# The last expert layer of a four-layer model: twelve token tiles sorted by expert, and router products over repeated columns

## The reference

```python
h = h + _L0_ffn_ref(_layernorm(h), ...)     # 8 experts, the best 2 for each token
h = h + _L2_ffn_ref(_layernorm(h), ...)     # 8 experts, weights of the best 2
h = h + _L3_attn_ref(_layernorm(h), ...)
h = h + _L3_ffn_ref(_layernorm(h), tile_sigs, W, b)

def _L3_ffn_ref(x, tile_sigs, W, b):        # T = 8 experts of 256 x 256
    scores = jnp.einsum('bsd,td->bst', x, jnp.sign(tile_sigs))
    idx = jnp.argmax(scores, axis=-1)
    all_out = jnp.einsum('bsd,tde->bste', x, W) + b[None, None]
    return jnp.take_along_axis(all_out, idx[:, :, None, None], axis=2)[:, :, 0, :]
```

## Time and profile before

| | us |
|---|---|
| median of 3 runs (range) | 1774.62 (1773.55 to 1776.07) |
| the profiled execution | 1774.82 |
| its span, first to last instruction | 1773.0 |
| TensorE busy | 1641.9 (93%) |
| VectorE busy | 805.2 (45%) |
| ScalarE busy | 493.8 (28%) |
| GpSimd busy | 417.3 (24%) |
| mean granted clock of TensorE | 0.955 |

### The profile page before, as it was taken

The page is one execution under the profiler, slowest core; times in us unless marked ns, Lnnn a source line. Parts: engine busy times, 40 slices in busy tenths (PEclk is TensorE's granted clock), DMA queues, the critical chain, the costliest instruction groups (busy, mean ns, idle before and its releaser), DMA issues.

```text
span 1773.0 us, 22370 instructions
## 1 busy us (share of the span) xinstructions
PE 1641.9 (93%) x7846; PEld 1142.3 (64%) x7846; DVE 805.2 (45%) x1721; ACT 493.8 (28%) x959; POOL 417.3 (24%) x428
## 2 busy tenths in 40 slices
PE   5877688898899999999999999999999989998999
PEld 4532234337899999999996555778844455667444
DVE  3530688896411111111117771124765647674455
ACT  1243444451122222222215413114200045553000
POOL 0353777781211111111113000000100013331000
PEclk8998899996899999999999998999899999997999
DMA  5232444443436645221321002000000000000000
GB/s 171 64 103 89 118 116 89 100 97 131 173 125 213 242 175 198 102 113 51 144 70 44 1 0 81 1 8 40 1 1 1 23 25 1 1 1 1 12 18 21
DMA packets 59189, 131.38 MB, mean 74 GB/s; under 512 B 10579, under 2 KB 39284, under 8 KB 52404
## 3 DMA queue, kind: packets, MB, share of 16 engines
q1 hardware_dynamic: 55140, 119.19, 21.0%
q0 software_dynamic: 3936, 10.75, 1.8%
HBM read 198.58 MB, written 9.97 MB: 118 GB/s over the span
## 4 chain that ended last, share of the span: by engine, by line
PE 76%; DVE 12%; POOL 3%; issue 3%; SPq 2%; ACT 2%; DMA 2%; DVEq 0%; ACTq 0%; POOLq 0%
PE psum L723 41%; PE psum L1018 13%; PE psum L755 7%; PE psum L818 4%; DVE work L1716 3%; PE psum L733 2%; PE psum L934 2%; DVE work L1856 2%; DVE work L1855 1%; SPq L622 1%; DVE bst L1403 1%; POOL xn L1921 1%; POOL work L1943 1%; PE psum L1027 1%; DMA work<-in_txt 1%
## 5 line engine op out<-in xcount | busy, mean ns | idle before, releaser
L723 PE MATMUL psum<-work 128*128 128x128 f32 (+3 forms) x3400 | 470.4, 300 | 15.7 <-DMA work<-in_xp 15.7
L723 PEld LDWEIGHTS psum<-work 128*128 128x128 f32 x3400 | 440.0, 193 | 33.1 <-DMA work<-in_xp 15.7
L1018 PE MATMUL psum<-w_late,xn 128*128 128x512 f32 x544 | 240.9, 601 | 0.0
L1783 DVE TENSOR_TENSOR work<-sq,psum 128x512 f32<-128x512 f32 x82 | 56.4, 688 | 386.4 <-PE psum L723 386.4
L1018 PEld LDWEIGHTS psum<-w_late,xn 128*128 128x128 f32 x544 | 103.2, 192 | 127.8 <-issue 118.3
L1716 DVE TENSOR_TENSOR_SCAN work<-psum,work 128x414 f32<-128x414 f32 (+1 forms) x160 | 159.3, 1060 | 34.3 <-POOL work L1943 29.2
L818 PE MATMUL psum<-work,xn 128*128 128x408 f32 (+1 forms) x320 | 151.5, 580 | 23.5 <-POOL work L1943 22.9
L1943 POOL TENSOR_TENSOR work<-work 128x408 f32<-128x408 f32 (+1 forms) x160 | 160.9, 1041 | 49.4 <-PE psum L818 24.2
L1600 DVE SCALAR_TENSOR_TENSOR h<-psum,gate,h 128x256 f32<-128x256 f32 x272 | 119.3, 480 | 105.4 <-PE psum L1018 102.5
L1902 POOL TENSOR_TENSOR rs<-rs,power 128x4 f32<-128x4 f32 (+3 forms) x40 | 44.4, 1110 | 503.4 <-DVE rs L1410 497.1
L1213 ACT ACTIVATE psum<-work,a_neg 128x408 f32<-128x408 f32 (+1 forms) x160 | 100.3, 627 | 113.9 <-DVE work L1716 113.9
(11 more groups left out here) (265 smaller groups left out, 2018.3 us busy)
## 6 DMA issues: line engine op xcount, KB each, us to landing
work<-in_W SPq DMA_DIRECT2D x123, 1024.0 KB
work<-c_rows SPq DMA_DIRECT2D x48, 204.0 KB, 3.2
w_attn<-in_B SPq DMA_DIRECT2D x64, 128.0 KB, 2.4
work<-c_rows SPq DMA_DIRECT2D x32, 238.0 KB, 3.6
w_attn<-in_A SPq DMA_DIRECT2D x64, 64.0 KB, 2.2
w_attn<-in_A SPq DMA_DIRECT2D x32, 128.0 KB, 2.5
work<-y_rows SPq DMA_DIRECT2D x8, 512.0 KB, 7.5
w_late<-in_we SPq DMA_DIRECT2D x2, 2048.0 KB, 8.3
```

Source lines behind the costliest of these rows:

```text
L723: mm = pe.matmul(dst, lhs(k), rhs(k), start=(k == 0), stop=(k == parts - 1))
L1018: mm = pe.matmul(dst.rearrange("p (e n) -> p e n", e=2), xn[:, k, i * P:(i + 1) * P], w_last[:, 2 * q:2 * q + 2, k, :], start=(k == 0), st ...
L1783: dve.tensor_tensor(hm[:, j % 2, 4 * q:4 * q + 4, :].rearrange("p k n -> p (k n)"), sa[:, i % 2], A.at(("e3", j, q)), ALU.mult).then_inc(s ...
```

## The change

Three things change.

First, the last feed-forward part. Tiles 0 to 11 (the first six duos, which are complete before the attention's last chunk) are sorted by expert into 19 blocks of 128; tiles 12 to 16 stay dense. The norms of the first three groups go to fixed places of VectorE's attention loop (`NORM3`), their transposes to TensorE's (`LN3`), and all twelve normalised tiles are kept, in memory that the attention no longer needs, and written to HBM beside `h` as rows of 512 numbers (`xh_rows`). The router of the twelve tiles runs at batch 29, `rank` at batch 30, the inverse map ahead of the last chunk's `out3`. GpSimd gathers the 19 blocks (2 KB a row: normalised token and `h`). For each block TensorE transposes it, reads the expert's number into a register, and adds two products with this expert's weights and one with the bias; VectorE adds the result to the block's `h` part; GpSimd scatters the rows to `y_rows`. At the end one transfer inside HBM copies 12 tiles from `y_rows` to the output. The norms, transposes and logits of tiles 12 to 16 stand between blocks.

Second, the router's products of all three layers stream the eight columns 16 times, 128 columns instead of 8. The sixteen copies go to neighbouring places of the bank and later tiles write over them. The products of the inverse maps stream their columns 2 times in layer 0 (164 instead of 82) and 6 times in the last layer (114).

Third, some tables are computed on all 128 partitions instead of one, so that the bias of a block can be chosen by a product (`bone`, one column for each block).

The diff, cut to its core:

```diff
+WIDE = 16
+SORT_D = 6
+SORT_T = 2 * SORT_D
+BLOCKS3 = SORT_T + EXPERTS - 1
+XT3 = 3
+FETCH3 = [1, 2, 4, 4, 4, 4]
+SORTS = [(TILES, SLOTS, BLOCKS), (SORT_T, 1, BLOCKS3)]
+ROUTED = [(0, TILES), (0, TILES), (0, SORT_T), (SORT_T, TILES)]
+DENSE_D0 = {1: 0, 2: SORT_D}
 ...
+    xh_rows = nc.dram_tensor("xh_rows", (SORT_T * P, 2 * D), F32, kind="Internal").ap()
 ...
-        POWER3 = {CHUNK_B0[min(c for c in range(CHUNKS) if CHUNK_END[c] >= g1 * P) + 1]: g for g, (g0, g1) in enumerate(GROUPS)
-                  if g1 * P <= CHUNK_END[CHUNKS - 2]}
+        POWER3 = {CHUNK_B0[2] + 1: 0, CHUNK_B0[3]: 1, CHUNK_B0[4] - 1: 2}
+        NORM3 = {CHUNK_B0[3] + 1: 0, CHUNK_B0[3] + 2: 1, CHUNK_B0[4] + 1: 2}
+        LN3 = {CHUNK_B0[3] + 3: (0, 1), CHUNK_B0[3] + 4: (2, 3), CHUNK_B0[4] + 2: (4, 5)}
+        ROUTE3 = BATCH - AHEAD
+        LATE_NORM, LATE_LN, LATE_LOGITS = 2, 5, 9
 ...
+                if b == BATCH:
+                    A.plan(("inv", 1), (sem("slots_known"), 5))
+                    step("inv", 1)
                 plan_h("out3", L3A, c)
-                plan_ln_after(L3F, c, 2)
+            if b in LN3:
+                plan_ln(L3F, LN3[b])
+            if b == ROUTE3:
+                plan_logits(2)
+            if b == ROUTE3 + 1:
+                ...
+                step("rank", 1)
 ...
+        for j in range(BLOCKS3):
+            if j + XT3 - 1 < BLOCKS3:
+                plan_xT3(j + XT3 - 1)
+            A.plan(("ey3", j), (sem("y_kept"), BLOCKS + j + 1))
+            step("ey3", j)
+            if j == LATE_LN:
+                plan_ln(L3F, range(SORT_D, DUOS))
+            if j == LATE_LOGITS:
+                plan_logits(3)
 ...
@@ block.sync @@
-            for d in range(DUOS):
+            for k in range(GROUP):
+                ...
+                sp.dma_start(to[:, :, D:], h[:, k * n:(k + 1) * n, :]).then_inc(sem("x_stored"), 16)
+                sp.wait_ge(sem("nx"), TILES * L3F + (k + 1) * n)
+                sp.dma_start(to[:, :, 0:D], xtok3[:, k]).then_inc(sem("x_stored"), 16)
+            for r in range(2):
+                sp.wait_ge(sem(f"y_stored{r}"), 16 * ((BLOCKS + 1 - r) // 2 + (BLOCKS3 + r) // 2))
+            sp.dma_start(out[0:SORT_T * P], y_rows[0:SORT_T * P]).then_inc(sem("stored"), 16)
+            for d in range(SORT_D, DUOS):
@@ block.tensor @@
-                    mm = product(dst[:, i * EXPERTS:(i + 1) * EXPERTS], lambda k: xn[:, k, i * P:(i + 1) * P],
-                                 lambda k: w[:, k, :], HALVES)
+                    mm = product(dst[:, i * EXPERTS:(i + WIDE) * EXPERTS].rearrange("p (r e) -> p r e", e=EXPERTS),
+                                 lambda k: xn[:, k, i * P:(i + 1) * P],
+                                 lambda k: w[:, k, :].unsqueeze(1).to_broadcast([P, WIDE, EXPERTS]), HALVES)
 ...
+                        wide, n = (2, 6)[s], (2 - s) * blocks
+                        mm = pe.matmul(dst[:, 0:wide * n].rearrange("p (r n) -> p r n", n=n), hot,
+                                       rows.unsqueeze(1).to_broadcast([P, wide, n]), start=(g == 0), stop=(g == slots * tiles - 1))
 ...
+            def xT3_(j):
+                pe.wait_ge(row3(FETCH_OF[j]), row3_loaded(FETCH_OF[j]))
+                dst = A.wait_free(pe, ("xT3", j))
+                for m in range(HALVES):
+                    tr = pe.transpose(dst[:, m * P:(m + 1) * P], xh[:, j, m * P:(m + 1) * P], ident[:])
+                tr.then_inc(sem("xT_done"), 1)
+
+            def ey3(j):
+                ...
+                e = pe.value_load(blk[0:1, 0, j:j + 1], min_val=0, max_val=EXPERTS - 1)
+                dst = A.wait_free(pe, ("ey3", j))[:, 0:D]
+                pe.wait_ge(sem("xT_kept"), BLOCKS + j + 1)
+                for k in range(HALVES):
+                    pe.matmul(dst, xT3[:, j % XT3, k, :], w_last[:, bass.DynSlice(e, 1), k, :].rearrange("p e n -> p (e n)"),
+                              start=(k == 0), stop=False)
+                pe.matmul(dst, bone[:, j:j + 1].to_broadcast([P, P]), be3[:], start=False, stop=True).then_inc(
+                    sem("ey_done"), 1)
@@ block.scalar @@
+            for j in range(BLOCKS3):
+                keep_xT3(j)
+                if j == LATE_LN + XT3 - 1:
+                    ln(L3F, range(SORT_D, DUOS))
@@ block.vector @@
+                if b in NORM3:
+                    norm(L3F, NORM3[b])
+                if b == ROUTE3:
+                    router(2)
+            for j in range(BLOCKS3):
+                dve.wait_ge(sem("ey_done"), BLOCKS + j + 1)
+                dve.tensor_tensor(xh[:, j, D:], xh[:, j, D:], A.at(("ey3", j))[:, 0:D], ALU.add).then_inc(sem("y_kept"), 1)
+                if j == LATE_NORM:
+                    norm(L3F, 3)
+                    norm(L3F, 4)
+                if j == LATE_LOGITS:
+                    router(3)
             dense(2, L3F)
@@ block.gpsimd @@
+            pool.wait_ge(sem("x_stored"), 16 * (len(GROUPS) + 2 * GROUP))
+            pool.wait_ge(sem("slots_known"), 4)
+            for j in range(BLOCKS3):
+                ...
+                pool.indirect_dma_start(xh[:, j], None, xh_rows, bass.IndirectOffsetOnAxis(
+                    row_of[:, 0, j:j + 1], 0)).then_inc(row3(g), 16)
+                if j == LATE_LOGITS:
+                    ln(L3F, range(len(POWER3), len(GROUPS)))
+            pool.wait_ge(sem("slots_known"), 5)
+            for j in range(BLOCKS3):
+                pool.wait_ge(sem("y_kept"), BLOCKS + j + 1)
+                pool.indirect_dma_start(y_rows, bass.IndirectOffsetOnAxis(row_of[:, 1, j:j + 1], 0), xh[:, j, D:],
+                                        None).then_inc(sem(f"y_stored{(BLOCKS + j) % 2}"), 16)
```

More of the change, by code:

```diff
@@ L854, in gateT, with rank @@
                     tr.then_inc(sem("gateT_done"), 1)
-            def rank():
-                pe.wait_ge(sem("chosen"), 1)
+            def rank(s):
+                tiles = SORTS[s][0]
+                ring = (Q, A)[s]
+                pe.wait_ge(sem("chosen"), s + 1)
                 pe.wait_ge(sem("prim_loaded"), 10 * 16)
-                dst = Q.wait_free(pe, ("rank",))
-                pe.matmul(dst[:, 0:TILES * EXPERTS], before[:], gate[:, 4], start=True, stop=True)
-                dst = Q.wait_free(pe, ("count",))
-                pe.matmul(dst[:, 0:TILES * EXPERTS], ones[:], gate[:, 4], start=True, stop=True).then_inc(sem("ranked"), 1)
@@ new lines, in rank, with inv @@
+                pe.matmul(dst[:, 0:tiles * EXPERTS], before[:], gate[:, 4, 0:tiles], start=True, stop=True)
+                dst = ring.wait_free(pe, ("count", s))
+                pe.matmul(dst[:, 0:tiles * EXPERTS], ones[:], gate[:, 4, 0:tiles], start=True, stop=True).then_inc(
+                    sem("ranked"), 1)
+            def inv(s):
+                tiles, slots, blocks = SORTS[s]
+                if s == 0:
+                    pe.wait_ge(sem("weights_placed"), 1)
+                dst = (Q, A)[s].wait_free(pe, ("inv", s))
+                for k in range(slots):
+                    pe.wait_ge(*placed(s, k + 2))
+                    for i in range(tiles):
+                        g = k * tiles + i
+                        hot, rows = ((onehot[:, k, i, :], in_block[:, g].rearrange("p a j -> p (a j)")) if s == 0 else
+                                     (onehot3[:, i, :], in_block3[:, i, :]))
+                        wide, n = (2, 6)[s], (2 - s) * blocks
+                        mm = pe.matmul(dst[:, 0:wide * n].rearrange("p (r n) -> p r n", n=n), hot,
+                                       rows.unsqueeze(1).to_broadcast([P, wide, n]), start=(g == 0), stop=(g == slots * tiles - 1))
+                mm.then_inc(sem("inverted"), 1)
@@ new lines, in places @@
+                for k in range(slots):
+                    dve.tensor_tensor(onehot[:, k] if s == 0 else onehot3, q_of[:, k].unsqueeze(2).to_broadcast([P, tiles, P]),
+                                      count_up.unsqueeze(1).to_broadcast([P, tiles, P]), ALU.is_equal).then_inc(
+                        sem("placed"), 1)
+                link(dve.tensor_tensor(bcmp[:, J], last.unsqueeze(1).to_broadcast([P, blocks_n, EXPERTS]),
+                                       count_up[:, J].unsqueeze(2).to_broadcast([P, blocks_n, EXPERTS]), ALU.is_le))
```

264 lines of the change are left out of this document (160 added, 104 removed).

## The result

The changed kernel took 1728.14 us (median of four, 1722.00 to 1732.72) against 1775.34 for the kernel before, a ratio of 0.973 (0.970 to 0.975). The forecast was 1703, with a range up to 1727. The profiled execution took 1732.72 us.

What follows compares the result with a forecast made beforehand. TensorE was taken to carry 76% of the chain of waits, with 132.7 us in one layer's dense experts. The terms summed to -71.9 us from 1774.8, or 1702.9, forecast as 1703 us, range 1686 to 1727.

Steps and rivals of the forecast that it cites:

- The blocks' stretch: Last layer's 19 sorted blocks: 29.3 us, plus 3.3 for late norm and logits and 3.8 for register reads.
- 1.54 us a block: Last layer, TensorE's price per block: two transposes (0.22) and three products of 256 columns (1.32).
- the 3.8 us for register reads: Last layer's blocks: reading the expert's number on TensorE's queue, 0.2 us a block, together 0 to 14.3.
- theory R: Follow-up forecast for w2: register reads hold TensorE's signals back; without them 19 blocks in 30 us, total -15 us (1713).
- rival 1: Last layer's blocks are paced by exposed reads or gathers of twice the bytes: +10.5 us, 1713; chance 13%.
- The norms in the attention: Last attention: two norm groups of 1.38 us moved behind VectorE's soft-max work, +2.8 us (0 to +5).
- Layer 0: Wide columns in logits (-6.5), logits to count product (-1.5) and inverse map (-1.8): sum -9.8 us.
- All of it lies on the chain: Layer 0: the whole -9.8 us from wide columns was claimed to lie on the chain of waits.
- Layer 2: Wide logits columns bring TensorE's clock back after 5 us: -4.5 us (+1.1 to -8).
- rival 2: Layers 0 and 2: wide columns buy nothing, idle time ahead decides the clock: +22.7 us, 1726; chance 6%.
- The bridge: From the last attention's end to the first block, 32.2 us before: -4.1 us (0 to -7).
- Rivals 3 to 5: Last layer: blocks at 1.2 GHz (1732, 6%); output copy ends last (1716, 5%); blocks don't overlap (1810, 4%).

Runs made afterwards that it cites:

- w2: Changed kernel with the last layer's blocks taking a fixed expert (j mod 8), without the 19 register reads or choice of expert: 1725.58 us.
- sets 1, 2 and 4: Groups of kernels measured together on one chip, with late signals; the unchanged new kernel took 1728.14 us in the first and 1727.18 in the last.
- w4: Changed kernel with the last layer's 19 gathers replaced by plain loads of the same bytes on SyncE's queue, rows unsorted: 1710.45 us.
- c2: Changed kernel with layer 0's loads later, attention norms ahead of the sum, and last-layer gathers paced by the blocks from the tenth on: 1719.99 us.
- w3: Changed kernel with the last layer's gathers fetching 1 KB rows instead of 2 KB, residual half left out: 1726.78 us.
- sets 4 and 6: Two later groups of kernels measured together, in which the changed kernel was run again without edits: 1727.18 and 1713.75 us.
- set 6: Last group of kernels measured together, without late signals; the unchanged new kernel took 1713.75 us there.
- after_third: The changed kernel without edits, measured a third time as a control: 1713.75 us.
- w1: Changed kernel with layer 0's seven weight loads waiting until two blocks are transposed: 1722.02 us.
- w7: Changed kernel with narrow columns again in the logits of layers 0 and 2 and layer 0's inverse map: 1719.90 us.
- w5: Changed kernel with each last-layer gather from the tenth on waiting until block j-7 is transposed: 1713.73 us.
- w6: Changed kernel with GpSimd clearing 512 elements and waiting, about 0.6 us, between two last-layer gathers: 1717.92 us.

## Why the prediction was wrong, step by step

The forecast against the two profiled executions, by stretch; "first" ran with delays (1732.72 us), "third" without (1709.53). A number is the difference to the forecast's own term.

| stretch | forecast | first | third |
|---|---|---|---|
| up to layer 0's router, unchanged code | 0 | +2.2 | 0.0 |
| layer 0, change of its 523.7 us | -9.8 | +6.8 | +4.1 |
| layer 1, unchanged | 0 | +0.1 | +0.5 |
| layer 2 to the attention's part at 1561.7 | -4.5 | +0.4 | -1.5 |
| from there to the end of the wide logits | 50.4 us | +6.4 | +5.4 |
| logits' end to the blocks' first transpose | 24.7 us | -0.6 | -1.2 |
| blocks with late norm and logits | 36.4 us | +14.7 | -0.4 |
| dense tiles to the chain's end | 40.0 us | -0.2 | -0.2 |
| sum | 1702.9 us | +29.8 | +6.7 |

**The blocks' stretch** failed, by half of the miss. "1.54 us a block" was right as a price (1.52 measured), the 3.8 us for register reads were hidden altogether (w2 took 1725.6 without them; theory R had expected 1713), and rival 1's mechanisms, exposed reads or slow gathers, don't show. What is missing in the sum is the way from TensorE's product to VectorE and ScalarE: I took it as immediate. In sets 1, 2 and 4 it took up to 13.4 us (12.6 in the first trace) while GpSimd's indirect transfers went out, and the waits cost TensorE its clock as well:

```profile
1641.00:1650.00 9.00, 7.76 (x31) 6.32 (x32) 0.84 (x2) 1.15 (x3) 7.27 (x9) 0.81 0.58 174
1650.00:1664.00 14.00, 4.82 (x23) 3.19 (x21) 3.25 (x9) 1.61 (x5) 8.55 (x10) 0.74 0.51 153
1664.00:1670.00 6.00, 5.70 (x16) 4.29 (x15) 0.42 (x1) 1.45 (x5) 2.70 (x3) 0.50 0.14 55
```

In these three stretches of the first trace TensorE (first column behind the length) is busy for 18.3 of 29 us, 4.8 of 14 in the second, and then runs 6 us at 0.50. w4 shows that without the gathers the delay is gone, c2 that it can come beside scatters alone, w3 that half the gathers' bytes change nothing, and the returns of the same kernel in sets 4 and 6 that the code alone doesn't decide. Why the signals are late stays open. The trace of before could not have told: behind the first five, GpSimd's gathers in layer 0 wait for blocks of 10.8 us each. In set 6, without delays, the same term is off by 0.4 us. That is partly luck: the 3.8 us for reads weren't there, and waits that the sum doesn't have, 1.4 us of them for a group of gathers, filled their place.

**The norms in the attention** were mis-sized: +2.8 forecast, 8.2 to 9.2 if the whole excess of their stretch is put to them. The term took 1.38 us from the earlier trace rows, a moment without GpSimd. Behind the batch's sum it is 2.56, twice, and 1.92 more of the third group on the chain. "Their transposes sit in TensorE's gaps: 0" was wrong as well: 1.30 us of transposes (1.71 at 1.2 GHz in the first trace), ScalarE's copy of 0.49 and another 1.08 of transposes stand on `after_third`'s chain, since the logits wait for them.

**Layer 0** was right up to the gather: from the router's statistics to the first gather 60.6 us became 52.0 in the first trace and 50.6 in the third, -8.6 and -10.0 against -9.8. The inverse map took 12.75 and 11.16 us (11.5 forecast). "All of it lies on the chain" was wrong. Seven weight loads are released by TensorE's next work; before, they left at 472.79, 2.8 us behind the first gather's issue, now at 465.27, 1.7 us behind it:

```profile
463.60 1.23 POOL L2114 DMA_INDIRECT work<-x_rows,row_of  x1 [14.60 <-DVE slot_of L1678]
465.14 0.95 POOL L2114 DMA_INDIRECT work<-x_rows,row_of  x1 [0.30 <-issue]
```

```profile
465.27 0.34 SPq L657 DMA_DIRECT2D w_attn<-in_win  x1
```

The second gather shared the transfer engines with them and took 5.98 us instead of 2.8 (5.01 in the third trace); block 0's products stand behind block 1's transpose. TensorE, idle for 6 us, began them at half clock (8.76 us for 64 passes). w1 shows the load part: 2.76 us again, layer 0 at 517.5 to 517.8 in all five traces with that edit, 517.9 to 521.0 in those without it (and with wide columns). The loads are not all. In `after_third` the 10.0 us at the gather became 5.7 at the layer's end: 2.2 went to the gather, 1.1 to block 0's products (8.43 us for 7.29 before, and 8.89 in w1's trace, where the gather was quick), and 1.1 behind the layer, where VectorE's second addition of the experts' sums took 1.80 us for 0.69 before, now beside a sum on GpSimd.

**Layer 2** was right (-4.1 and -6.0 for -4.5), and so was the mechanism of the wide columns; rival 2 (they buy nothing) falls with w7. **The bridge** was right in sum with other parts: placing on VectorE took 7.2 us from the rank product on as forecast (7.1), the inverse map 5.45 at half clock instead of 3.7, but the projection 8.8 instead of 11. I had not seen that the gathers are signalled in groups: the fourth block waited for the seventh gather, 1.4 us in `after_third`, part of the blocks' 36.0. **Rivals 3 to 5**: the blocks ran at 2.4 GHz where they weren't stopped; the output's copy took 6.8 us and ended long before the dense tiles; nothing came near slower.

The range missed for the median by 1 us. It was built from independent prices, and the largest miss is not a price but a delay that no row of before has.

## What to carry to other kernels

Time that a faster stage saves is kept only if the transfers it releases don't meet the next stage's: look at what each saved microsecond starts, not only at what it ends. Work moved into another engine's busy stretch costs what it costs beside that engine's neighbours, so take its duration from such a moment. And a single trace, or a single set, can't price an edit of 10 us here: the control belongs into every set, or w5 and w6 would have passed for cures.

## What was not expected of the hardware

TensorE's signals reached VectorE and ScalarE up to 13.4 us late in three of six sets, where GpSimd issued indirect transfers one behind the other, every 1.25 to 1.28 us (gathers in most traces, scatters alone in c2's), and on the first trace's chain nowhere else; the same kernel then took 1727 or 1728 us instead of 1714. Reading a number from on-chip memory into a register of TensorE's queue took 0.30 us, with 0.15 of arithmetic behind it, and cost nothing behind queued products. The Trainium skill ("DMA: Bandwidth & Descriptors", Latency and other measured facts) gives about 600 ns as the floor of such a load; here the trace has half of it.
